# A graph-and-expert layer: SyncE no longer fetches six blocks row by row; GpSimd gathers all 782

## The reference

```python
xn = _layernorm(x)
# graph convolution (its heart; the kernel's middle part)
h = xn @ W
dinv = rsqrt(segment_sum(edge_weight, dst) + 1)
norm = dinv[src] * edge_weight * dinv[dst]
agg = segment_sum(norm[:, None] * h[src], dst) + (dinv * dinv)[:, None] * h
h = layernorm(agg + b) * gamma + beta
gnn = relu(0.5 * h + 0.5 * xn)
# linear attention over all nodes, 8 heads: q, k = elu(.) + 1
mix = ((q @ (k.T @ v)) / (q @ k.sum())) @ Wproj.T + bproj
x = x + gnn + mix
# 16 experts, the best 2 of each node, 256 -> 512 -> 256
x = x + layernorm(xn2 + moe(xn2)) * gamma2 + beta2      # xn2 = layernorm(x)
```

## Time and profile before

| | |
|---|---|
| median of 3 runs | 2265.05 us (2261.67 to 2266.09) |
| profiled execution, first to last instruction | span 2246.5 us |
| TensorE busy, share of the span | 1583.4 us, 70% |
| VectorE busy | 1134.0 us, 50% |
| GpSimd busy | 1042.0 us, 46% |
| ScalarE busy | 486.3 us, 22% |
| mean granted TensorE clock | 0.817 |

### The profile page before, as it was taken

One profiled execution on the slowest core, in us unless ns is written; L12 is line 12 of the kernel. 1 busy time (PEld: TensorE's weight loads), 2 busy tenths in 40 slices (PEclk: granted clock), 3 DMA queues, 4 the chain that ended last, 5 costly groups with the idle time before them and its releaser, 6 DMA issues. The chain is left out here.

```text
span 2246.5 us, 37994 instructions
## 1 busy us (share of the span) xinstructions
PE 1583.4 (70%) x7988; PEld 1272.2 (57%) x7989; DVE 1134.0 (50%) x4097; ACT 486.3 (22%) x1376; POOL 1042.0 (46%) x1093
## 2 busy tenths in 40 slices
PE   8998355576556666665567655475756899999997
PEld 5676344455445445444445444354544699998885
DVE  8997233443334444443444333443446655556559
ACT  4444110111101111110111110111102444444434
POOL 1323455544445545444544545454540355554556
PEclk9999676777777777777777776777777999999999
DMA  6106222222222222222222222222225522224338
GB/s 224 38 30 159 72 76 69 74 60 71 68 66 73 71 68 71 67 75 66 75 62 69 73 71 71 71 70 58 79 71 116 158 82 91 91 90 157 119 112 305
DMA packets 131263, 201.58 MB, mean 90 GB/s; under 512 B 49798, under 2 KB 86028, under 8 KB 131180
## 3 DMA queue, kind: packets, MB, share of 16 engines
q0 software_dynamic: 47952, 131.12, 20.0%
q1 hardware_dynamic: 82940, 68.92, 10.3%
q10 hardware_dynamic: 288, 0.66, 0.1%
HBM read 166.97 MB, written 34.39 MB: 90 GB/s over the span
## 5 line engine op out<-in xcount | busy, mean ns | idle before, releaser
L135 POOL DMA_INDIRECT ring<-table,src x776 | 736.8, 950 | 750.3 <-PE bank L1153 418.9
L1153 PE MATMUL bank<-ring,late_hots 128*128 x384 | 156.3, 573 | 361.9 <-SPq L814 232.8
L1153 PE MATMUL bank<-ring,hots 128*128 x1372 | 340.7, 406 | 94.5 <-remote 70.9
L1153 PEld LDWEIGHTS bank<-ring,hots 128*128 128x128 f32 x1372 | 279.4, 206 | 148.7 <-issue 106.0
L1153 PEld LDWEIGHTS bank<-ring,late_hots 128*128 128x128 f32 x384 | 105.0, 287 | 405.7 <-issue 387.9
L1091 ACT ACTIVATE xn<-x,half_s,half_r (+1 forms) x48 | 28.8, 600 | 1071.5 <-PE bank L1244 450.0
L1686 PEld LDWEIGHTS bank<-one,w 128*128 128x128 f32 x1696 | 205.0, 192 | 10.1 <-issue 3.8
L1686 PE MATMUL bank<-one,w 128*128 128x128 f32 x1696 | 207.4, 275 | 1.6 <-issue 1.1
L1694 PE MATMUL bank<-w,one 128*128 128x256 f32 x848 | 203.0, 381 | 6.2 <-DVE y L1758 4.7
L1659 ACT ACTIVATE one<-bank,b 128x128 f32<-128x128 f32 x424 | 142.8, 366 | 232.5 <-PE bank L1686 203.5
L1605 POOL DMA_INDIRECT spread<-y,to_x x109 | 108.2, 993 | 169.2 <-DVE y L1758 75.4
(11 more groups left out here) (294 smaller groups left out, 2507.0 us busy)
## 6 DMA issues: line engine op xcount, KB each, us to landing
w<-in_w SPq DMA_DIRECT2D x32, 512.0 KB
ring<-table,src POOLq DMA_INDIRECT x776
side<-table SPq DMA_DIRECT2D x768, 1.0 KB
got<-spread SPq DMA_DIRECT2D x11, 1024.0 KB, 9.7
rows<-xn SPq DMA_DIRECT2D x1, 6272.0 KB, 25.4
out<-xn SPq DMA_DIRECT2D x12, 512.0 KB, 5.8
xt<-in_x_cols SPq DMA_DIRECT2D x11, 512.0 KB, 3.5
table<-xn SPq DMA_DIRECT2D x5, 896.0 KB, 6.3
```

The lines of the kernel that those rows point to most:

```text
L135: return pool.indirect_dma_start(out=m.ring[:, b % RING, :], out_offset=None, in_=a.table, in_offset=bass.IndirectOffsetOnAxis(ap=m.src[:, ...
L1153: last = nc.tensor.matmul(agg, hot[:, k, :], two[:, k, :], start=False, stop=False)
```

## The change

`BY_ROWS` is empty in effect: its constants, the buffers `row_src` and `side`, the semaphores `picked`, `row_in` and `side_in`, and the functions `fetch_row` and `send_block` go. GpSimd gathers all blocks from 4 to 781, and SyncE's program in this stage is a loop of relays.

```diff
         def _(sp):
             with sp.If(out_of_order(sp)):
                 sp.wait_ge(rg.again, 16 * GATHERED_AHEAD)
-            for k, b in enumerate(BY_ROWS):
-                sp.dma_start(a.row_src[k][:, None], m.src[:, b:b + 1]).then_inc(picked, 16)
-            sp.wait_ge(picked, 16 * len(BY_ROWS))
...
-            def relay(step):
-                sp.wait_ge(landed[step % 8], by_pool(step) * 16)
-                for k, b in enumerate(BY_ROWS):
-                    if b // 4 == step:
-                        sp.wait_ge(side_in, k * 16 + 16)
+            for step in range(FULL // 4):
+                sp.wait_ge(landed[step % 8], (step // 8 + 1) * 64)
                 sp.sem_inc(gathered, 2)
-
-            def fetch_row(k, r):
-                row = sp.value_load(row_src[0:1, r:r + 1])
-                row = nc.s_assert_within(row, 0, NP - 1, skip_runtime_bounds_check_because="an index of a row of x")
-                sp.dma_start(a.side[k, r:r + 1], a.table[bass.ds(row, 1)]).then_inc(row_in, 16)
-
-            def send_block(k):
-                b = BY_ROWS[k]
-                sp.wait_ge(freed, (b + 2 - RING) // 2 + CREDIT)
-                sp.dma_start(ring[:, b % RING, :], a.side[k]).then_inc(side_in, 16)
-
-            for k in range(len(BY_ROWS)):
-                sp.dma_start(row_src[:], a.row_src[k:k + 1]).then_inc(picked, 16)
-                sp.wait_ge(picked, 16 * (len(BY_ROWS) + k + 1))
-                if k > 0:
-                    sp.wait_ge(row_in, k * (P * 16))
-                r = 0
-                for step in range(GROUPS):
-                    if k > 0 and step == SENT:
-                        send_block(k - 1)
-                    relay(k * GROUPS + step)
-                    while r < (step + 1) * P // GROUPS:
-                        fetch_row(k, r)
-                        r += 1
...
             for k in range(FULL % 4 // 2):
-                sp.wait_ge(landed[FULL % RING // 4], by_pool(FULL // 4 - 8) * 16 + 32 * (k + 1))
+                sp.wait_ge(landed[FULL % RING // 4], FULL // RING * 64 + 32 * (k + 1))
                 sp.sem_inc(gathered, 1)
...
             for b in range(GATHERED_AHEAD, FULL):
-                if b in BY_ROWS:
-                    continue
                 if b >= RING and b % 4 == 0:
                     pool.wait_ge(freed, (min(b + 4, FULL) - RING) // 2 + CREDIT)
```

More of the change, by code:

```diff
@@ L39 @@
 FULL = NB - 2
-ROWS_EVERY = 116
-BY_ROWS = [ROWS_EVERY * (k + 1) + 38 for k in range(6)]
 PAIRS = NB // 2
@@ L700, in layers @@
         mark = sb("mark", [P, 1])
-        row_src = sb("row_src", [1, P], I32)
         score = sb("score_l", [P, E])
@@ L718, in layers @@
             "chain", "chain_rs", "chain_h", "chain_x1", "chain_top", "both_ok", "turn_ok", "start_ok"))
-        picked, row_in, side_in = map(sem, ("picked", "row_in", "side_in"))
         moments_ok, momtr_ok, momT_ok, ctx_ok, ctxT_ok, attend_mm = map(sem, (
@@ L798, in _ @@
                 sp.wait_ge(rg.again, 16 * GATHERED_AHEAD)
-            for k, b in enumerate(BY_ROWS):
-                sp.dma_start(a.row_src[k][:, None], m.src[:, b:b + 1]).then_inc(picked, 16)
-            sp.wait_ge(picked, 16 * len(BY_ROWS))
[L802 to L807, removed]
-            def relay(step):
-                sp.wait_ge(landed[step % 8], by_pool(step) * 16)
-                for k, b in enumerate(BY_ROWS):
-                    if b // 4 == step:
-                        sp.wait_ge(side_in, k * 16 + 16)
-                sp.sem_inc(gathered, 2)
@@ L839, in _ @@
-            sp.wait_ge(row_in, len(BY_ROWS) * P * 16)
-            for step in range(GROUPS * len(BY_ROWS), FULL // 4):
-                if step == GROUPS * len(BY_ROWS) + SENT:
-                    send_block(len(BY_ROWS) - 1)
-                relay(step)
+            for step in range(FULL // 4):
+                sp.wait_ge(landed[step % 8], (step // 8 + 1) * 64)
+                sp.sem_inc(gathered, 2)
             for k in range(FULL % 4 // 2):
-                sp.wait_ge(landed[FULL % RING // 4], by_pool(FULL // 4 - 8) * 16 + 32 * (k + 1))
+                sp.wait_ge(landed[FULL % RING // 4], FULL // RING * 64 + 32 * (k + 1))
@@ L1996 @@
     a.edges = nc.dram_tensor("edges", (NEP, 3), F32).ap()
-    a.side = nc.dram_tensor("side", (len(BY_ROWS), P, D), F32).ap()
-    a.row_src = nc.dram_tensor("row_src_d", (len(BY_ROWS), P), I32).ap()
     a.rows = nc.dram_tensor("rows", (NP, D + 2), F32).ap()
```

## The result

| | changed kernel | kernel before |
|---|---|---|
| median on the same chip | 2134.13 us (4 runs, 2130.31 to 2151.11) | 2265.57 us (4 runs, 2261.67 to 2272.95) |
| ratio, with its 95% interval | 0.9427 (0.9386 to 0.9469) | |
| profiled span | 2128.4 us | 2246.5 us |

The change makes the kernel 5.7% faster on this chip; 2144 us was forecast. The chip of this table is called **chip F** from here on. Its number isn't on record, so it isn't known whether it is a fifth chip or one of the four at another time. The ratios of the tables compare runs in the fast state alone, which leaves out one of e9's seven runs, 2427.86 us at a granted clock of 0.549.

A forecast was written before the change was run, and what follows sets the result against it. SyncE's row fetches were taken to bound 300 to 1570 us; turn 2 at 328 plus 44 turns of 27.8 us, 121 us gained, span 2125, median 2144 us. Own range 2085 to 2180, 8 in 10 1985 to 2205.

The forecast's parts named there:

- SyncE late by 40 us, and free afterwards: SyncE's relays: row fetches between them make them about 40 us late; without the fetches, relays follow landings at 3 us.
- the 21 to 25 blocks of the prediction: Ring: blocks gathered but not relayed, 25 at 600 us and 21 at 1400 us, read as about 40 us of lateness.
- A row at 1.75 us: SyncE's queue: each of 768 row fetches with its register load takes 1.75 us, 7.7 us a relay, 30.9 us for 16 blocks.
- The stretch from 673 to 683.6 us: SyncE's row fetches: nine in a stretch taken as quiet, some 1.3 us each.
- The free turn of 27.8 us: Turns once SyncE is free: 27.8 us each from three cycles near the fetches' end, against 30.8 before, over 44 turns.
- The 3 us: Within a turn: TensorE's completions held until some 3 us after a GpSimd burst, then 5.4 us until the next pairs are free.
- Turn 2 at 328: Start of the turns: turn 2 has its mark at 328 instead of 333.2 us; the start before it doesn't change.
- GpSimd's idle time before gathers of some 600 us: GpSimd: idle time before gathers falls from 750 to some 600 us, still partly waiting for freed slots.
- Median 2144: Whole kernel: profiled span of 2125 us plus the 18.6 us between span and median, let stand from the kernel before.
- The six gathers at 1.25 us: GpSimd: six gathers added at 1.25 us each, 7.5 us together, counted as part of the 782 blocks.
- A: Rival: TensorE's hold goes too, GpSimd alone bounds at 20 us a turn, some 1800 us; chance 0.09.
- C's "simpler case": Slower rival's second case: SyncE isn't late in a timed run and six gathers add 7.5 us; chance 0.06 with C.

The follow-up runs named there:

- e9: The changed kernel with 2 MB copied from DRAM to DRAM in each turn, issued by ScalarE: 1738.13 us, 1.0046 of the kernel before without traffic.
- e6: The kernel before with two more row fetches behind each relay, into a buffer nobody reads: 1978.56 us, 1.1435 of the kernel before.
- e8: The kernel before with 2 MB copied from DRAM to DRAM in each turn, issued by ScalarE: 1841.20 us, 1.0658 of the kernel before without traffic.
- e12: The kernel before with three spread row blocks, 2.2 rows a relay, and 2 MB copied in each turn: 1732.32 us, 1.0033 of the kernel before without traffic.
- e7: The kernel before without an edit, run on chip 0 for its trace: 1729.89 us in one run.
- e5: The changed kernel without an edit, timed on chip 0: 1737.14 us, 1.0039 of the kernel before.
- e11: The kernel before with three row blocks instead of six, spread over the whole stage, 2.2 rows a relay: 1731.86 us, 1.0024 of the kernel before.
- e1: The kernel before with three row blocks instead of six, GpSimd gathering the other three: 1731.95 us, 1.0011 of the kernel before.
- e10: The changed kernel with 5 MB copied from DRAM to DRAM in each turn: 1837.75 us in one run, against 1728.10 us for the kernel before without traffic.
- e4: The changed kernel with GpSimd waiting after every 8 gathers until they have landed: 1962.42 us, 1.1354 of the kernel before.
- The first four experiments: Chip 11: three row blocks, register loads without row DMAs, DMAs from fixed rows, the changed kernel with pauses; 1731.95, 1728.44, 1728.84, 1962.42 us against 1728.39.
- e3: The kernel before with its 768 row DMAs from fixed rows and no register loads: 1728.84 us, 1.0002 of the kernel before.

## Why the prediction was right, and where it holds

**SyncE late by 40 us, and free afterwards: right on chip F.** Relays follow the gathers at 3 us, TensorE's wait for relays has left the page, and the lag is none. It was larger than the 21 to 25 blocks of the prediction, which left the blocks by rows out of one of the two counts: GpSimd had passed block 154 by 600 us and five of the six by 1400 us, so it was 26 blocks ahead at both times. That a queue is late by what it issues between two relays is shown apart from chip F by e6 (made late by two rows more) and e8 (made late by a slower row); e12 shows the reverse.

**A row at 1.75 us: right as a mean, with a reading that hides the cause.** The stretch from 673 to 683.6 us isn't quiet, as the prediction has it: five gathers start in it. SyncE's row DMAs of the kernel before on chip F, first from 654.8 to 672.8 us, where GpSimd gathers 12 blocks up to 669.5 us, then from 704.5 to 714.7 us, where it gathers none:

```profile
L819 SPq DMA_DIRECT2D side<-table x6: 12/596/700, 655.0 to 672.4; - x6
...
L819 SPq DMA_DIRECT2D side<-table x10: 483/492/493, 705.1 to 714.0; - x10
```

Ten rows without gathers are 0.99 us apart, six with them 3.5 us. So it is in the whole trace from 300 to 1568 us: more than 3 us behind a burst's last gather, 245 rows begin in 244 us, 1.00 us each as on chip 0; while GpSimd gathers, 367 rows take 797 us, 2.2 us each. The time isn't in the DMA instruction, which takes 458 ns in the mean on chip F from 300 to 1050 us and 496 in e7. It is in the register work (the two instructions behind the load take 300 ns in the mean there and 66 in e7) and between the instructions. So the slow rows that bound SyncE and the stretched free turn go with one and the same condition: on chip F the instructions of TensorE, VectorE and SyncE stretch while GpSimd gathers. That GpSimd's gathers cause it was not tested there. The prediction had seen the register instruction of 700 ns, but counted the two as separate costs.

**The free turn of 27.8 us: 28.35.** This was the step held most likely to fail. It is 2% short: 44 x 0.55 is 24 us too much gain. Its parts came out otherwise than written: h starts 5.7 us behind the burst and not 3, and the next burst 0.8 us behind that mark and not 5.4; the sum of the two, 6.5 us, and the other pauses of 7.8, 8.7 and 9.7 us lie around the 8 us that the mean over whole cycles had. The 3 us are found again in `xn`, on which the next products and so the next burst wait. `h` isn't on that path, so counting from it was an accident of the turn in the earlier trace rows, in which VectorE and ScalarE started together.

**Turn 2 at 328: 310.1 us.** The start is 18 us better than forecast, since the relays had cost time there already: the sum held that SyncE wasn't late enough to count at 281 to 305 us. In the trace of before, SyncE's first relay comes at 224.7 us, 15 us later than in the changed kernel (209.9 us), which has no index loads ahead of it, and the sixth comes 41 us behind the start of its group's last gather already. This step failed, by 18 us, and nearly makes up for the one above, which is luck: turn 46 was forecast at 1554 us (1551, and 3 for the long last cycle) and stands at 1557.5.

**GpSimd's idle time before gathers of some 600 us: 621.0. Span 2125: 2128.4. Median 2144: 2134.13.** The difference of 18.6 us between span and median was let stand; for the changed kernel it is 5.7 us. It isn't time around the span, which is 1.8 to 1.9 us in every run that has both on record; the profiled execution of the kernel before, at some 2248 us, was faster than its timed runs (2261.67 to 2272.95). So the gain forecast at 121 us is 118 us between the two spans and 131 us between the medians.

**The six gathers at 1.25 us.** Right, and measured apart: 6.7 to 8.2 us for six (e5), 4.2 to 4.9 us for three (e11); e1's 1.9 to 3.6 us for three isn't clear of noise. On chip F they are part of the 28.35 us turn and can't be told apart; on the four chips without traffic they are the whole effect.

**The rivals.** None came about on chip F. On the four numbered chips, A's turn of 20 us and C's "simpler case" came about together: the hold is gone, for the kernel before as well, and the change loses by its six gathers. What gave this 0.09 and part of 0.06 was a premise that the prediction never wrote down: that the times of SyncE's register work and TensorE's hold are the kernel's, and not the chip's. The rule of the Trainium skill that was weighed there (page "SBUF — State Buffer", section "SBUF: two separate sides", transfers and engines don't share ports) agrees with the traces of the four chips: 19.5 us a turn in e7 with h 0.4 us behind the close. On chip F the turn isn't the 20 us that the rule was taken to give, with a hold of some 16 us in most turns. That isn't shown to speak against the rule itself: what stretches there are instructions, SyncE's register work among them, and whether a port has any part in it no run shows.

**What stays open.** What chip F's state is, and why the other engines' instructions stretch in it while GpSimd gathers. It isn't the row fetches (the changed kernel has none and is held), nor is it brought about by traffic from another queue (e10). Gathers don't take longer to land there: the relay comes 2.7 to 2.9 us behind the last gather's start in the changed kernel on chip F and in e5. It can't be said whether it belongs to that chip, to other work beside it, or to a time, since it didn't come again in the twelve traces from four chips. Whether e4's pauses would shorten the hold there is untested for the same reason, and so is e11. The first four experiments were meant to take SyncE's cost apart on chip F and say nothing on it.

## What to carry to other kernels

Before removing helper work from a queue that also passes on signals, write down its comparison: items per signal times us per item, against the pace of the producer; here 4.41 rows at 1.00 us lie 12% below the point, and one slow neighbour on the DMA queues (1.28 us) tips it. An engine that relays signals should have a margin for its DMA instructions' tail, as with 2.2 rows. And where a profile shows the same cheap instruction at 37 ns and at 700 ns, time the kernel on a second chip, or at another time, before tuning to it: the change takes 5.7% off in one condition and adds 0.4% in the other, and the signs of the other (1728 us before, gathers without a stop) are those of all four chips of the experiments.

## What the hardware showed that was not expected

**One program, two conditions.** The same program takes 2265 us on chip F and 1727 to 1729 us on chips 11, 0, 13 and 3. Of the changed kernel's 391 us between chip F and e5 (spans of 2128.4 and 1737.4 us), 359 lie in the 44 turns from 2 to 46, 28.35 us each against 20.19. TensorE's granted clock explains little of that: TensorE's busy time is 1560.1 us on chip F and 1513.7 in e5, 46 us more. On chip F instructions that handle semaphores and registers grow on VectorE, and in the kernel before on SyncE, while GpSimd gathers; ScalarE's semaphore instructions stay at 17 ns. VectorE's semaphore instructions from 400 to 1500 us in the changed kernel on chip F, and from 400 to 1100 us in e5 on chip 0:

```profile
L188 DVEq EVENT_SEMAPHORE  x655: 2/21/1411, 400.1 to 1497.6; - x164
```

```profile
L188 DVEq EVENT_SEMAPHORE  x594: 21/21/50, 400.5 to 1097.8; - x198
```

The median is the same 21 ns; the longest is 1411 against 50 ns. With it goes the hold of TensorE's completions: in the median of the turns `xn` starts 15.8 us behind the record of TensorE's close on chip F and 0.7 us behind it in e5.

**The granted clock is lower where TensorE is less busy.** In the turns it is 0.73 on chip F, with TensorE busy for 64% of the time, and 0.90 on chip 0, with 84%; behind the turns it is 0.96 on chip F, with 90%. The stretches from 310 to 1550 us of the changed kernel on chip F and from 310 to 1150 us of e7:

```profile
310.00:1550.00 1240.00, 798.39 (x3276) 607.30 (x3276) 544.43 (x2260) 149.39 (x436) 676.30 (x708) 0.73 0.26 75
```

```profile
310.00:1150.00 840.00, 704.07 (x3159) 551.99 (x3158) 532.51 (x2192) 149.61 (x417) 636.38 (x669) 0.90 0.39 107
```

**A row DMA's issue has a tail.** With the row's address from a register it takes 492 ns in the median of every trace. The longest are 1.0 to 1.2 us on the four chips without other traffic (e7, e1, e11, e6), 1.4 us on chip F, and 6.06 us with 2 MB a turn from another engine's queue (e8). With a fixed address the median is 590 ns (e3). An indirect gather's issue on GpSimd doesn't grow in the median by any of this: 946 to 949 ns in every trace.
